# Expert stage: rows read in 32-column pieces and turned by VectorE, weights first in two queues, six output banks

## The reference, cut to what matters

```
packed = buf[:E * capacity].reshape(E, capacity, d)        # E = 16, capacity 1280, d = 256
h = jax.nn.gelu(jnp.einsum('ecd,edf->ecf', packed, w1) + b1[:, None, :], approximate=False)   # f = 1024
expert_out = jnp.einsum('ecf,efd->ecd', h, w2) + b2[:, None, :]
out = gathered * gate, summed over the token's two experts
```

## Time and profile before

| | |
|---|---|
| median of 3 runs | 3318.99 us (3316.73 to 3319.85) |
| profiled execution, its own time | 3325.69 us |
| its span, first to last instruction | 3323.9 us |
| experts, first layer (first up to last out) | about 303 to 1282 us |
| experts, second layer | about 2317 to 3312 us |
| mean granted TensorE clock | 0.962 of full speed |

### The profile page before, as it was taken

The page is one execution under the profiler, slowest core; times in us unless marked ns, Lnnn a source line. Parts: engine busy times, 40 slices in busy tenths (PEclk is TensorE's granted clock), DMA queues, the critical chain, the costliest instruction groups (busy, mean ns, idle before and its releaser), DMA issues. The chain is left out here.

```text
span 3323.9 us, 63196 instructions
## 1 busy us (share of the span) xinstructions
PE 2899.8 (87%) x22656; PEld 2337.1 (70%) x22656; DVE 2005.2 (60%) x4425; ACT 1337.9 (40%) x2281; POOL 1695.3 (51%) x1510
## 2 busy tenths in 40 slices
PE   4453999999999995899999999974999999999997
PEld 4453888888888883466756666664888888888886
DVE  4343555555555653577888888753555555565563
ACT  3341444444444442343444444421444444444442
POOL 2543554554545443356676767644345445454543
PEclk9999999999999997899999999965999999999998
DMA  9813333343333324601111111002333334334334
GB/s 305 285 67 103 75 81 81 74 86 78 76 83 87 77 51 115 208 15 37 35 48 34 47 34 47 27 31 94 78 76 82 81 73 86 84 72 88 81 66 136
DMA packets 231849, 281.02 MB, mean 85 GB/s; under 512 B 18999, under 2 KB 214651, under 8 KB 231520
## 3 DMA queue, kind: packets, MB, share of 16 engines
q1 hardware_dynamic: 173760, 203.16, 20.3%
q0 software_dynamic: 57888, 75.16, 12.9%
HBM read 142.44 MB, written 146.41 MB: 87 GB/s over the span
## 5 line engine op out<-in xcount | busy, mean ns | idle before, releaser
L688 ACT ACTIVATE be_h<-be_pH,b 128x512 f32<-128x512 f32 (+1 forms) x384 | 237.2, 618 | 555.5 <-PE be_pH L623 483.1
L688 ACT ACTIVATE ae_h<-ae_pH,b 128x512 f32<-128x512 f32 (+1 forms) x384 | 237.2, 618 | 539.8 <-PE ae_pH L623 487.8
L714 POOL DMA_INDIRECT acc_a<-ae_ob,ae_to x160 | 254.9, 1593 | 94.1 <-POOL ae_ob L706 66.7
L706 POOL TENSOR_SCALAR ae_ob<-ae_ob,ae_gate 128x256 f32<-128x256 f32 x160 | 174.3, 1191 | 247.5 <-DVE ae_ob L829 247.5
L714 POOL DMA_INDIRECT acc_b<-be_ob,be_to x150 | 238.4, 1589 | 88.2 <-POOL be_ob L706 62.3
L706 POOL TENSOR_SCALAR be_ob<-be_ob,be_gate 128x256 f32<-128x256 f32 x150 | 163.0, 1183 | 222.4 <-DVE be_ob L829 222.4
L1461 POOL TENSOR_TENSOR m_xf<-m_tmp,m_xT 128x512 f32<-128x512 f32 x160 | 181.3, 1159 | 119.3 <-DVE m_tmp L1182 119.1
L434 POOL DMA_INDIRECT slots_a<-ar_row,ar_sidx x128 | 125.9, 984 | 158.7 <-issue 150.3
L1514 POOL DMA_INDIRECT slots_b<-m_row,m_sidx x128 | 152.9, 1195 | 84.0 <-issue 84.0
L1756 PEld LDWEIGHTS m_PP<-m_RP,m_KS 64*64 64x64 f32 x6656 | 121.1, 139 | 88.4 <-issue 87.3
L1756 PE MATMUL m_PP<-m_RP,m_KS 64*64 64x64 f32 x6656 | 135.7, 226 | 37.6 <-DVE m_A L1212 36.5
(11 more groups left out here) (342 smaller groups left out, 9384.7 us busy)
## 6 DMA issues: line engine op xcount, KB each, us to landing
ae_stage<-in_w SPq DMA_DIRECT2D x64, 512.0 KB
be_stage<-in_w SPq DMA_DIRECT2D x64, 512.0 KB
slots_a<-empty SPq DMA_DIRECT2D x10, 2080.0 KB, 19.7
ae_xp<-slots_a SPq DMA_DIRECT2D x80, 260.0 KB
slots_b<-empty SPq DMA_DIRECT2D x10, 2080.0 KB, 19.2
be_xp<-slots_b SPq DMA_DIRECT2D x80, 260.0 KB
ar_xin<-in_x SPq DMA_DIRECT2D x16, 512.0 KB, 5.8
acc_a<-ar_xin SPq DMA_DIRECT2D x16, 512.0 KB
```

The costliest lines, as they stand in the source:

```text
L688: t = act.activation(dst[:, 0:SIZES[b]], pH[c % 2][:, 0:SIZES[b]], ACT.Gelu, bias=S.b1[:, bass.ds(i * (2 * FC) + (u * FC + f), 1)])
L706: t = pool.tensor_scalar(ob[m][:, q, :], ob[m][:, q, :], gate[m][:, q:q + 1], None, ALU.mult)
L714: pool.indirect_dma_start(S.acc[tag][:, :], bass.IndirectOffsetOnAxis(ap=to[m][:, q:q + 1], axis=0), ob[m][:, q, :], None, bounds_check=T ...
```

## The change

- The rows of a block are no longer read as whole 1040 B rows. `load` issues eight DMAs for a block, one for each 32-partition quarter j and each half k of the 256 columns; a piece is 32 columns (128 B) of one row. The piece of slot 32n+i goes to partition 32j+i of `xq[b]`, so each 32x32 square only has to be turned in itself. The last four words of the rows come by a DMA of their own into `tails`.
- `turn` on TensorE and `pT` go. VectorE turns a unit with one transpose instruction (128x512, `xq` to `x32`), and the high and low parts are made from `x32` in SBUF.
- The two banks of `pT` go to `pO`, now three tiles of two banks; unit m has tile HOME[m] = 0, 1, 2, 0, 1, and `emptied` follows.
- VectorE does `split_h` before `out`, and one unit's `out` in f = 1, the other in f = 2. `weights_low` stands in (0,2), (0,4), (0,7), (1,4).
- GpSimd casts parts 0 and 1 of the next weights when the last `up` of the expert before is done, ahead of `send` of unit 4, and parts 2 and 3 right behind it.
- SP issues parts 0 and 1, then block 0, tails, bias, parts 2 and 3, blocks 1 and 2. At a stage's start block 0 stands ahead of the weights.

```
-        xp = [sb(f"xp{m}", [P, 2, ROW]) for m in range(UNITS)]
+        xq = [sb(f"xq{b}", [P, DC, SIZES[b]]) for b in range(BLOCKS)]
+        tails = [sb(f"tails{u}", [P, 2 * UNITS, ROW - D]) for u in range(2)]
+        x32 = [sb(f"x32_{r}", [P, DC, BS]) for r in range(2)]
-        pT = [ps(f"pT{r}", [P, DC, BS]) for r in range(2)]
-        pO = ps("pO", [P, 4, 2 * D])
+        pO = [ps(f"pO{r}", [P, 2, 2 * D]) for r in range(3)]
+        HOME = (0, 1, 2, 0, 1)
...
+        x_d = S.slots[tag].rearrange("(e n i) d -> e i n d", n=CAP // BLK, i=BLK)
...
+                def load(i, u, b):
+                    m = units(b)[-1]
+                    if due(i * NU + (u - 1) * UNITS + m + 1):
+                        sp.wait_ge(xp_free, i * NU + ((u - 1) * UNITS + m + 1))
+                    e = i * 2 + u
+                    n0, n1 = b * FULL // BLK, (b * FULL + SIZES[b]) // BLK
+                    for j in range(QUADS):
+                        for k in range(DC):
+                            cs = slice(k * P + j * BLK, k * P + j * BLK + BLK)
+                            sp.dma_start(xq[b][j * BLK:(j + 1) * BLK, k, :].rearrange("i (n d) -> i n d", d=BLK),
+                                         x_d[e][:, n0:n1, cs]).then_inc(xq_loaded[b], 16)
+
+                def load_tails(i, u):
+                    if due(i * NU + (u - 1) * UNITS):
+                        sp.wait_ge(xp_free, i * NU + (u - 1) * UNITS)
+                    sp.dma_start(tails[u][:, :, :], tail_d[i * 2 + u][:, :, D:ROW]).then_inc(tails_loaded[u], 16)
...
+                load(0, 0, 0)
                 for k in range(2):
                     weights(0, 0, k)
-                for m in range(2):
-                    load(0, 0, m)
+                load_tails(0, 0)
...
-                for m in units(0):
-                    turn(0, 0, m)
...
-                    if b == 0:
-                        return u * UNITS - 1 - j
-                    return u * UNITS + m - 2
+                    before = [k for k in range(m) if HOME[k] == HOME[m]]
+                    if before:
+                        return u * UNITS + before[-1]
+                    return (u - 1) * UNITS + [k for k in range(UNITS) if HOME[k] == HOME[m]][-1]
...
+                    dve.transpose(x32[n % 2][:, :, :], xq[b][:, :, ts]).then_inc(turned, 1)
                     dve.wait_ge(turned, i * NU + n + 1)
...
-                    dve.tensor_copy(xT[r][HI][:, :, ts], pT[n % 2][:, :, :]).then_inc(xT_high, 1)
+                    dve.tensor_copy(xT[r][HI][:, :, ts], x32[n % 2][:, :, :]).then_inc(xT_high, 1)
...
+                        split_h(i, c)
+                        if f in (1, 2) and not (first and c < FC):
                             u0, b0, _ = place(c - FC)
-                            for m in units(b0):
+                            for m in units(b0)[f - 1:f]:
                                 out(i if c >= FC else i - 1, u0, m)
```

More of the change, by code:

```diff
@@ L483, in experts @@
         b2_loaded = [sem(f"b2_loaded{u}") for u in range(2)]
-        xp_loaded = [sem(f"xp_loaded{m}") for m in range(UNITS)]
+        xq_loaded = [sem(f"xq_loaded{b}") for b in range(BLOCKS)]
+        tails_loaded = [sem(f"tails_loaded{u}") for u in range(2)]
         stored = [sem(f"stored{m}") for m in range(UNITS)]
@@ L556, in bias @@
                     sp.dma_start(b2[u][:, :], S.b2[i * 2 + u].partition_broadcast(P)).then_inc(b2_loaded[u], 16)
+                load(0, 0, 0)
                 for k in range(2):
                     weights(0, 0, k)
-                for m in range(2):
-                    load(0, 0, m)
+                load_tails(0, 0)
                 for k in range(2, 4):
                     weights(0, 0, k)
-                for m in range(2, UNITS):
-                    load(0, 0, m)
+                load(0, 0, 1)
                 bias(0, 0)
-                for m in range(2):
-                    load(0, 1, m)
+                load(0, 0, 2)
                 def step(i, first, last):
@@ L573, in step @@
                             i1, u1 = (i, 1) if u == 0 else (i + 1, 0)
-                            weights(i1, u1, 0)
+                            for k in range(2):
+                                weights(i1, u1, k)
+                            load(i1, u1, 0)
+                            load_tails(i1, u1)
                             bias(i1, u1)
[L576 to L583, removed]
-                            for m in units(0):
-                                load(i + 1, u, m)
+                            for k in range(2, 4):
+                                weights(i1, u1, k)
+                            load(i1, u1, 1)
+                            load(i1, u1, 2)
                 loop_with_ends(sp, E // 2, step)
@@ L597, in _ @@
             def _(pe):
[L598 to L607, removed]
                 passes = [(HI, HI), (HI, LO), (LO, HI)]
@@ L664, in step @@
                             down(i, c - LAG)
[L665 to L669, removed]
                     if last:
@@ L755, in step @@
                         more = not (last and u == 1)
+                        if more:
+                            if due(i * NCH + u * CH):
+                                pool.wait_ge(up_full, i * NCH + u * CH)
+                            for k in range(2):
+                                weights_high(i1, u1, k)
                         if not (first and u == 0):
@@ L760, in step @@
                                 pool.wait_ge(chunk_down, i * NCH + u * CH)
-                            for k in range(2):
+                            for k in range(2, 4):
                                 weights_high(i1, u1, k)
@@ L764, in step @@
                             send(i, u, m)
-                        if more:
-                            for k in range(2, 4):
-                                weights_high(i1, u1, k)
                         for m in units(1):
@@ L850, in step @@
                         u, b, f = place(c)
-                        if f == 1 and not (first and c < FC):
+                        split_h(i, c)
+                        if f in (1, 2) and not (first and c < FC):
                             u0, b0, _ = place(c - FC)
-                            for m in units(b0):
+                            for m in units(b0)[f - 1:f]:
                                 out(i if c >= FC else i - 1, u0, m)
@@ L856, in step @@
                                     merge(m)
-                        split_h(i, c)
                         u1, b1, over = after(u, b)
@@ L862, in step @@
                                 split_x(i + 1 if over else i, u1, units(b1)[j])
-                        if b < 2 and f in (4, 7) and not (last and u == 1):
-                            weights_low(i if u == 0 else i + 1, 1 - u, 2 * b + f // 7)
+                        if (b, f) in LOWS and not (last and u == 1):
+                            weights_low(i if u == 0 else i + 1, 1 - u, LOWS.index((b, f)))
                     if last:
```

38 lines of the change are left out of this document (21 added, 17 removed).

## The result

The changed kernel takes 3346.82 us (median of 4 runs, 3345.17 to 3353.41) where the kernel before takes 3319.42 beside it: a ratio of 1.0087, 95% interval 1.0073 to 1.0100. It is slower by 0.9%; I had forecast 3250 us. The profiled execution took 3347.96 us, its span 3346.1, with a mean granted clock of 0.941 (before 0.962).

A forecast was written before the change was run, and what follows sets the result against it. TensorE was taken to bound the expert stages, working almost without a gap. Terms -69 - 38 + 16 + 15 + 10 = -66 took 3325.69 to 3260 us, 3253 at the runs' median, forecast 3250; range 3225 to 3288.

The forecast's parts named there:

- term 3: TensorE's wait for unit 4's banks in a new expert, its `out` now behind `split_h`: +16 us.
- term 2: TensorE's wait for `hT1l`, caused by GpSimd's late casts of w2, taken off entirely: 38 us less.
- Term 1: The turns: 156 turns of four transposes leave TensorE, 0.44 us each, 69 us less.
- Term 4: VectorE in the 256-slot block: longer `split_x` makes low parts late for TensorE, 0.5 us 30 times, +15 us.
- Term 5: Start of a stage: SP issues block 0's eight DMAs ahead of the weights, two stages of 5 us, +10 us.
- Pieces: Loading x as 128 B pieces: DMA share rises from 0.37 to about 0.5, nothing waits, 0 us.
- the second: Rival: pieces of x fill the DMA engines, every load is late, about 3375 us; chance 0.06.
- GpSimd slowed by VectorE's reads: Sign that the forecast is wrong: VectorE's new SBUF reads slow GpSimd, so casts are late at (0,2); no size.

The follow-up runs named there:

- unit 4 sent first: Changed kernel, but GpSimd sends unit 4 before casting parts 0 and 1, and VectorE's low parts return to their old places; ratio 0.9781 to the kernel before.
- early turns: Changed kernel with `out` of unit 4 before `split_h`, first x block from ScalarE's queue, next expert's first two units turned at (1,6), (1,7); 0.9566 of the kernel before.
- half on x: Changed kernel's x pieces, VectorE turns and six banks only; weights queue, casts, `out` and low parts in the old order; ratio 1.0363 to the kernel before.
- half casts: Changed kernel, but from the second expert pair GpSimd casts only 512 of 1024 columns of parts 0 and 1; ratio 0.9824 to the kernel before.

## Why the prediction was wrong

The step that failed is **term 3**, +16 us. It prices TensorE's wait for the banks of unit 4. Its sum gave VectorE 0.61 us for the `split_h` ahead of `out` of unit 4, "a 128x512 instruction to the start of the next", as if the row held in any company. I had moved the casts in term 2 and priced them nowhere as neighbours. Measured, the wait is 85.3 us in two stages for the forecast 36, against 18.3 before: +67 us. On top comes the clock. The changed kernel and the one with unit 4 sent first run the same 4864 matmuls in stage a:
```profile
300.00:1290.00 990.00, 935.27 (x4864) 791.01 (x4864) 636.64 (x1080) 433.14 (x769) 518.88 (x376) 0.97 0.44 76
```
```profile
262.00:1197.00 935.00, 912.11 (x4864) 773.03 (x4863) 629.26 (x1077) 433.14 (x769) 505.97 (x376) 1.00 0.47 80
```
Of the 55 us between them 32 are waits (54.7 and 22.9 us idle) and 23 are slower matmuls at the lower clock. Twice 23 on top of 67 makes term 3 about +113 us, 97 more than forecast. That the distance from 3250 to 3347 is the same number is chance: the errors of the other terms about cancel.

The sign stood in the earlier trace rows: beside the two casts of w2 the low part took 2.04 us, and the median of its group is 1.22. I read it as VectorE's time, not as time it was held. By the Trainium skill, "SBUF — State Buffer", section "Who interferes with whom", an instruction of VectorE with two inputs in SBUF contends with one of GpSimd that reads SBUF, one in a two-port mode with any of GpSimd's, and the later blocks until the other ends. The trace agrees on which instructions are held; by the profile's start times it differs on who is: `split_h` starts 0.15 us before the cast (615.32, 615.47) and is the one held. At 620.15 it is the other way round. GpSimd's scaling starts 0.31 us ahead of VectorE's low part, which takes its usual 1.22 us, and the two scalings take 3.14 us. In the kernel before, at the place of the earlier trace rows, they take 2.09, and 2.23 with unit 4 sent first, both times with no low part beside them:
```profile
620.15 3.14 POOL L702 TENSOR_SCALAR ae_ob<-ae_ob,ae_gate 128x256 f32<-128x256 f32 x2 [2.09 <-DVE ae_ob L833]
620.46 1.22 DVE L781 TENSOR_TENSOR ae_w_0l<-ae_stage,ae_w_0h 128x1024 fp32r<-128x1024 f32 x1
```
```profile
614.93 2.09 POOL L706 TENSOR_SCALAR ae_ob<-ae_ob,ae_gate 128x256 f32<-128x256 f32 x2 [1.82 <-DVE ae_ob L829]
```
So the order of starts in the profile doesn't say who is held; what does is open.

- **Term 1** (-69): the transposes are gone. Without the meeting the period is 58.2 us (553.59 to 611.88 to 670.02, unit 4 sent first), where I had said 58.4.
- **Term 2** (-38): right for the wait for w2; the groups of `hT1h` wait 0.0 us in place of 38.5. Two waits of these 38.5 (4.03 and 2.04 us, in the last expert of stage b) weren't for w2, and 6.45 us stand there before `hT3l` now.
- **Term 3 without the meeting**: 0.81 us of wait measured for 1.0 worked out.
- **Term 4** (+15): the transpose takes 0.70 us (said 0.69), the cast 0.43 undisturbed (0.55). From its first up matmul to the next expert's, a 256-slot block takes 13.64 us in the mean where it took 14.06 with two turns of 0.44, so TensorE loses 0.46 us there per expert, close to the 0.5 of the term. With the early turns the block takes 12.72. For the cast the estimate from "VectorE: DVE Perf Modes" in the Trainium skill, 0.42, was nearer than my 0.55.
- **Term 5** (+10): from the last row that VectorE makes in the routing (258.3, before 267.2) to the first matmul of stage a it is 43.5 us in place of 36.0; in stage b, from the end of the last `slots` scatter, 22.6 in place of 15.5: +14.5.
- **Pieces** (0): share 0.45 for "about 0.5"; by the run of the half on x the cover hangs on the queue's new order, which I had not named as the condition.

A count from start to start closes the sum; idle times alone don't, since the ends of matmuls are modelled. It takes the 28 experts that are neither first nor last in a stage, and measures each block from its first up matmul to the next block's (means of both stages). The first 512-slot block takes 25.84 us for 22.39, the second 22.60 for 24.60, the 256-slot block 13.64 for 14.06. They held two, one and two turns of 0.44. With the turns given back, that is +121 us for term 3, -44 for term 2 and +13 for term 4, beside -62 of turns. The first block takes 22.05 in the run with unit 4 sent first. So 106 of the 121 are the meeting with the clock behind it, and the 15 that are left are the 16 of the forecast. The first and last experts of the stages give -15, the starts +14.5, and two stretches that the change doesn't touch -8.9 (the routing of the first layer) and +2.8 (between the stages, the start aside). Together +22, and the spans differ by +22.2.

Of the rivals, the second had the sign and not the cause: DMA never filled. My list of what would make it wrong named GpSimd slowed by VectorE's reads, so that casts come late. GpSimd was slowed, the scalings from 1.19 to 1.48 us in the mean, but VectorE's low parts wait at most 1.0 us in stage a for its casts in place of 102. What cost the time was the same meeting with the roles exchanged, and I gave it neither price nor chance.

## What to carry to other kernels

When work moves to another time on GpSimd, list what VectorE does at that time and which of it reads SBUF twice or copies SBUF to SBUF: price each as held for the whole of what GpSimd does there (the half casts cost less, 0.56 us, and GpSimd may be the one held), and look at what stands behind it in VectorE's order. Let PSUM readers meet it, or an instruction with slack, rather than the one TensorE waits for. A reorder that loses by itself can pay together with another: each half of this change alone cost about 4%, both together 0.9%, and with one instruction moved it gained 3%.

## What the runs showed of the hardware

Durations on VectorE in stage a of the changed kernel (ns: least, median, most), by where the inputs lie:
```profile
L833 DVE TENSOR_TENSOR ae_ob<-ae_pO,ae_ob x80: 690/691/693, 331.4 to 1289.2; 128x512 f32<-128x512 f32 x80
...
L816 DVE TENSOR_TENSOR ae_hT1l<-ae_h,ae_hT1h x96: 415/692/3511, 308.6 to 1284.2; 128x512 fp32r<-128x512 f32 x64, 128x256 fp32r<-128x256 f32 x32
...
L810 DVE TENSOR_TENSOR ae_gate<-ae_gate,ae_tails x80: 148/162/2374, 299.7 to 1266.1; 128x2 f32<-128x2 f32 x80
```
With PSUM as one input the spread is 3 ns; with both in SBUF an instruction of 0.16 us can take 2.4. The stream transpose, one SBUF input, was never held (697 to 708 ns in stage a), but only 13 of its 160 instructions in both stages had a cast or scaling of GpSimd beside them; the SBUF-to-SBUF cast was (426 to 2545). And a wait of 2.20 us on TensorE (at 557.73) already brought the lower clock for 3 to 4 us, while waits of 0.8 us never did, nor did the 1.66 us that the kernel before waits at 1021.68. In the run of the half on x one of 2.73 us (at 696.9) brought none.
